# Where a step's third value product stands: behind the key projection, or at the step's end

## The reference

```python
def local_layer(x):                                  # x: 512 x 128 (one sequence)
    q, k, v = split(shift(x) @ Wqkv)                 # 16 heads of width 64
    q, k = rotary(l2norm(q) * qs), rotary_inv(l2norm(k) * ksc)
    sim = 8 * q @ k.T                                # in windows of 32 queries, 64 keys, masked
    x = x + (softmax(sim) @ v) @ Wo
    h = layernorm(shift(x)) * g + b
    a, gate = split(h @ W1 + b1)                     # 2 x 341
    return x + (a * gelu(gate)) @ W2 + b2
```

## Time and profile before

| | us |
|---|---|
| median of 3 runs | 1943.56 (1942.86 to 1945.3) |
| the profiled execution | 1939.44 |
| its span, first to last instruction | 1937.7 |
| TensorE matmuls busy | 1792.5 (93%) |
| VectorE busy | 1538.9 (79%) |
| ScalarE busy | 1360.8 (70%) |
| GpSimd busy | 1280.3 (66%) |

### The profile page before, as it was taken

The page is one execution under the profiler, slowest core; times in us unless marked ns, Lnnn a source line. Parts: engine busy times, 40 slices in busy tenths (PEclk is TensorE's granted clock), DMA queues, the critical chain, the costliest instruction groups (busy, mean ns, idle before and its releaser), DMA issues.

```text
span 1937.7 us, 60121 instructions
## 1 busy us (share of the span) xinstructions
PE 1792.5 (93%) x24400; PEld 1025.6 (53%) x24400; DVE 1538.9 (79%) x2553; ACT 1360.8 (70%) x2863; POOL 1280.3 (66%) x1223
## 2 busy tenths in 40 slices
PE   5898989768999999999999999999999999999996
PEld 3343434355555555555555555555555555555552
DVE  4788888347888888888888888888888888888874
ACT  1354545447888778887787778887788877888771
POOL 4303020147888887887888887888878888878751
PEclk8899999889999999999999999999999999999998
DMA  8000000223533334333344333343333333333320
GB/s 178 27 2 2 2 1 2 66 50 78 114 75 72 79 81 93 86 73 73 75 90 98 76 68 81 81 92 85 73 81 81 89 74 73 85 74 73 70 47 22
DMA packets 137217, 132.64 MB, mean 68 GB/s; under 512 B 79336, under 2 KB 82984, under 8 KB 136616
## 3 DMA queue, kind: packets, MB, share of 16 engines
q1 hardware_dynamic: 136944, 128.81, 29.9%
HBM read 20.94 MB, written 1.05 MB: 11 GB/s over the span
## 4 chain that ended last, share of the span: by engine, by line
POOL 56%; issue 18%; PE 4%; DVE 1%; ACT 1%; POOLq 0%; DVEq 0%; ACTq 0%
POOL prob L1242 9%; POOL kfin L1270 6%; POOL kfin L1267 6%; POOL kfin L1266 6%; POOL qfin L1275 6%; POOL qfin L1274 5%; POOL sumq L1284 5%; POOL kfin L1271 4%; POOL sumk L1262 4%; POOL sumk L1263 3%; POOL lower L1280 1%; PE bank_z L867 1%; PE bank_y L875 1%; PE bank_a L856 1%; PE bank_z L917 0%
## 5 line engine op out<-in xcount | busy, mean ns | idle before, releaser
L1070 ACT ACTIVATE prob<-s_in,lower,rq 128x64 f32<-128x64 f32 x1536 | 537.8, 436 | 0.3
L856 PE MATMUL bank_a<-x_shift,wqk_sb 128*128 128x512 f32 x768 | 364.6, 597 | 5.9 <-ACT sq L1216 4.2
L1056 ACT ACTIVATE zT<-bank_z 128x1024 f32<-128x1024 f32 x192 | 193.1, 1019 | 72.7 <-PE bank_z L867 71.2
L1242 POOL TENSOR_TENSOR prob<-prob,rden 128x1024 f32<-128x1024 f32 x96 | 182.8, 1904 | 89.4 <-DVE rden L1338 83.6
L1270 POOL TENSOR_TENSOR kfin<-rk,kfin 128x512 f32<-128x512 f32 x96 | 122.4, 1275 | 147.9 <-ACT rk L1197 92.6
L856 PEld LDWEIGHTS bank_a<-x_shift,wqk_sb 128*128 128x128 f32 x768 | 144.5, 191 | 139.9 <-issue 127.5
L385 ACT ACTIVATE a_prob<-a_sT 128x1024 f32<-128x1024 f32 x128 | 130.7, 1025 | 103.4 <-PE a_sT L219 101.4
L494 DVE TENSOR_REDUCE a_negmax<-a_max 128x1 f32<-128x512 f32 x256 | 164.7, 685 | 47.9 <-PE a_max L169 44.2
L875 PE MATMUL bank_y<-zT,wvo_low 128*128 128x512 f32 x384 | 187.2, 610 | 0.7 <-ACT zT L1056 0.4
L875 PE MATMUL bank_y<-zT,wvo_high 128*128 128x512 f32 x384 | 187.2, 610 | 0.0
L867 PE MATMUL bank_z<-pT,xk_prev 32*128 32x128 f32 x3072 | 165.1, 284 | 11.3 <-DVE xn L1371 8.0
(11 more groups left out here) (203 smaller groups left out, 4057.9 us busy)
## 6 DMA issues: line engine op xcount, KB each, us to landing
kpad<-kfin SPq DMA_DIRECT2D x384, 128.0 KB, 2.4
qpair<-qfin SPq DMA_DIRECT2D x384, 128.0 KB, 2.4
wqk_sb<-in_wqkv SPq DMA_DIRECT2D x40, 128.0 KB, 2.6
xk_prev<-xk_own SPq DMA_DIRECT2D x24, 192.0 KB, 2.4
ffn_sb<-in_ffn SPq DMA_DIRECT2D x6, 537.5 KB, 4.1
wvo_low<-in_wqkv SPq DMA_DIRECT2D x6, 256.0 KB, 5.6
wvo_low<-in_wo SPq DMA_DIRECT2D x3, 512.0 KB, 6.7
wvo_high<-in_wqkv SPq DMA_DIRECT2D x6, 256.0 KB, 5.0
```

The costliest lines, as they stand in the source:

```text
L856: last = pe.matmul(bank_a[:, half, :], wqk_sb[:, layer_of(u) % 2, part, half, g * P:(g + 1) * P], cols(u), start=True, stop=True)
L1056: return act.activation(out, in_, ACT.Copy)
L1070: last = act.activation(prob[:, n % 2, i, :], s_in[:, n % 2, i, :], ACT.Exp, bias=lower[:, n % 2, i:i + 1], scale=rq[:, n % 2, i:i + 1])
L1242: pool.tensor_tensor(prob[:, e % 2], prob[:, e % 2], rden[:].unsqueeze(2).broadcast_to([P, TPB * GH, 2 * WIN]), ALU.mult).then_inc(pn_ok, 1)
```

## The change

The third value product (hh = 2) of a step moves from behind the key projection to the end of the step, ahead of the fourth. The first call then issues two products and the second call two. Each product is issued as two records. Nothing else changes: no instruction is added or removed, the order of the sums in `bank_y` is the same, and `y_mm` still comes with the fourth product.

```diff
@@ in TensorE's step(s)
                     if h % GROUPS == 0:
                         after(pe, xa_ok, h // GROUPS - 1)
-                    project_out(h, 0, 3)
+                    project_out(h, 0, 2)
...
                     weigh_rows(e)
                 if quarter(h):
-                    project_out(h, 3, 4).then_inc(y_mm, 1)
+                    project_out(h, 2, 4).then_inc(y_mm, 1)
                 if quarter(e):
                     after(pe, z23_ok, e)
```

## The result

The changed kernel takes 1962.19 us (median of 4 runs, 1961.19 to 1964.45), the kernel before 1944.12 us beside it (4 runs). The ratio is 1.0095, with a 95% interval of 1.008 to 1.0109: slower by 18 us. The forecast was 1945.0 us in 1938 to 1951, no change. It was wrong.

A forecast was written before the change was run, and what follows sets the result against it. TensorE's order was taken to set the step, except where other engines hold it. Units +4.2, first steps -3.9 and last steps +1.2 sum to +1.5 us; on a median of 1943.6 that gave 1945, range 1938 to 1951.

The forecast's parts named there:

- C: Third step kind of a four-step unit: sumk ready, 0.86 us kept, another 0.17 us of copy wait goes; -0.52 us.
- D: Fourth step kind of a unit: sumk not waited for, 0.86 us kept against +0.51 at the end; -0.35 us.
- A unit, +0.20: Four steps, one of each kind: +0.56 + 0.51 - 0.52 - 0.35 = +0.20 us; 21 units in steps 12 to 95, +4.2 us.
- A: First step kind of a unit: sumk just ready, no saving counted, L1422 0.05 us late; +0.56 us.
- B: Second step kind of a unit: TensorE already waits for sumk, all 0.86 us turns into waiting; +0.51 us.
- rival 3: In D, the chain from y_mm to L1422 is 0.25 us late instead of 0.05; +5.7 us, 1949; chance 0.10.
- The key sum as an anchor: At L969 in A and B: sumk's chain starts at TensorE's own tail, so the 0.86 us taken out becomes waiting.
- Rival 1: In A and B sumk comes forward, so every step saves the copy's wait; about 1908, half 1927; chance 0.12.
- Rival 2: At the step's end nothing is filled: the moved product costs 0.86 us in each tail; +34 us, 1976; chance 0.06.
- The first steps, -3.9: Steps 4 to 8 gain 3.0 us ahead of the key sum, steps 9 to 11 the rest; bounds 0 and -5.2.
- The last steps, +1.2: Step 96's moved product comes behind a 3.37 us wait, costing 1.0 us; steps 97 to 99 give +0.15.
- Rival 4, the clock: After longer waits in A and B TensorE returns at half clock once a unit; +57 us, 2001; chance 0.02.

The follow-up runs named there:

- before with its blocks moved (first and second): Kernel before plus satisfied waits and repeated score products, 24 then 15 repeats in step 13, shifting 256-instruction block ends: 1962.62 us (1.0079), then 1936.93 us (0.9953).
- VectorE's late order: Kernel before with VectorE's last hidden rows products and output additions put behind the key's products: 1944.8 us (0.9994).
- VectorE's queue cut: VectorE's L1422, L1428 and L1429 on 8 of 512 columns: in the kernel before 1918.61 us (0.9855), in the changed kernel 1911.62 us (0.9818).
- the two late runs: VectorE's last hidden rows products and output additions put behind the key's: in the kernel before 1944.8 us (0.9994), in the changed kernel 1954.85 us (1.0045).
- the mixed order: Kernel before with the third product moved in C and D only: 1943.01 us (0.9993); with block ends shifted, second try, 1929.27 us (0.9914).

## Why the prediction was wrong, step by step

**The step that failed: the sum.** It has terms for units, first and last steps, and treats what lies between the waits as fixed. The 9.6 us of irregular time in steps 12 to 94, pauses at the ends of blocks and the lower clock behind some, are in none of them. The kernel before had them too, in steps 43, 32, 15 and others, 3.7 us in its trace; I read the 1.00 of the earlier trace rows and the list of waits, where L889's 1.8 us of "issue" was too small to be asked about. The change hardly moves the ends: it carries four instructions past the scores, so the end of step 26 stands at 222 in place of 218, that of step 48 at 220 in place of 216. But there the trace of the kernel before has no pause, and that of the changed one 1.58 and 2.06 us, with a product of 0.86 us fewer ahead of the scores. With the ends moved away from the scores, the two orders compare as 1.0004 and 0.9953 of before, a difference of 0.5%, 9.9 us (each has an interval of 0.13 to 0.15%, on different chips; pauses ahead of step 12 are left in both). So of the 18 us about 10 are the order and about 8 the blocks: pauses cost the changed kernel 17.7 us by its runs (1.0095 to 1.0004) and the kernel before 9.1 (1 to 0.9953). Both are 4 to 5 us more than the traces show in steps 12 to 94 (13.0 and 3.7). For the kernel before one reason is that the profiled execution, 4 us faster than the median, was poor in pauses. Steps 4 to 12 are instruction for instruction the same in before, in before with its blocks moved (first and second), and step 10 has no pause in the first trace, 0.95 us in the second and 1.08 us in the third; from L958 of step 4 to that of step 12 they take 114.1, 115.6 and 117.7 us. And at the end 218 in step 26, where before has no pause, the same TensorE order paused 1.35 us with VectorE's late order and 0.84 us with VectorE's queue cut. So part of the 9.6 us between the two traces is chance of the execution; the 8 us rest on medians. That the missing product is what makes the same ends costlier is argued, not shown. For it: the irregular time grows wherever steps are shorter (11.5 us in C and D alone, 20.8 with VectorE's queue cut).

Between the two traces the forecast of +1.5 us and the measured +21.7 differ by 20.2 us: 9.6 irregular time in steps 12 to 94, 2.8 regular time there, 3.7 in the first steps, 2.4 in the last, and 1.7 ahead of step 3, which the change can't have made.

**A unit, +0.20: measured +0.32.** The signs and the kinds are right: A +0.65 (forecast +0.56), B +0.54 (+0.51), C -0.52 (-0.52), D -0.35 (-0.35). The term mis-sized is "two products take 1.72 us": behind `weigh_rows` they take 1.82, so the tail is 0.61 and not 0.51 later. The copy has no part in it, since it ends 0.23 us ahead of the tail's first weight load. The 0.10 us is in the first record behind `weigh_rows`, which the next follows after 0.53 us in place of 0.43, in both kernels; so a lone product there took 0.96 us, and the copy's wait was 1.21 - 0.96 = 0.25 and not 0.35 us. What comes behind the tail is 0.05 to 0.11 us shorter in return. In A `weigh_rows` also starts 0.09 us later: L1422 starts 0.73 us behind the start of the last linear record in place of 0.63, and now directly behind VectorE's own L1415. That is rival 3's chain, at the upper end of the forecast's 0 to 0.1 and not at the 0.25 of the rival. 21 x 0.32 = 6.7 in place of 4.2.

**The key sum as an anchor: right, with the wrong owner.** All 0.86 us turned into waiting in A and B. But the two late runs show that `sumk` can be made early without any gain; the hold is VectorE's queue, which starts at TensorE's own tail. Rival 1 needed this hold to give way and it did so only where VectorE had less to do. Rival 2 is out: C and D came as forecast. (Its 1976 us is 1975 by its own terms with the first and last steps, which changes nothing.)

**The first steps, -3.9: measured about 0.** From L958 of step 4 to that of step 12 it is 114.16 us after and 114.08 before. Steps 4 to 8 gained 0.9 us and not 3.0, with a pause of 0.50 ahead of the scores in step 5; step 10 was to gain 0.52 and lost 1.1, by a pause of 1.27 us. The pauses are half of the 3.7 us error. In the rest the prediction's lower bound came true (GpSimd's loop holds the period): around step 9 TensorE waits 0.34 and 0.55 us for `sumq` and 0.49 us in step 8 for `sumk`, where before has no such wait.

**The last steps, +1.2: measured +3.6** from step 95's L958 on. Step 95 is longer by 0.35. Most of the rest is the clock: the same six records of the last hidden products, in before (4.25 us) and in after (5.46 us):
```profile
1923.49 4.25 PE L1032 MATMUL bank_z<-hid,ffn_sb 128*128 128x512 f32 x6 [3.58 <-DVE hid L1422]
```
```profile
1944.00 5.46 PE L1032 MATMUL bank_z<-hid,ffn_sb 128*128 128x512 f32 x6 [3.58 <-DVE hid L1422]
```
The granted clock there was 0.65 and 0.50, behind the same wait; the six records some 20 us ahead took 2.74 us at 1.00 before and 4.44 at 0.62 after. What decides between the two was not found, and it changes by itself: two kernels that are the same from step 95 on (the change in C and D alone, without and with its blocks moved the second time) took 90.2 and 87.7 us from step 95's L958 to the end.

**Rival 4, the clock:** it came, but in single steps. The 1.45 us waits of step B left the clock at 1.00 in all units but one (step 17, 0.95 us lost); in the trace of the change in A and B alone the lower level came behind the same waits in four (steps 41, 49, 61 and 73, some 0.9 to 1.0 us each). So one such spell costs about 1 us and not the 2.7 of the rival. Behind the pauses of 1.58 and 2.06 us in steps 26 and 48 it fell (behind that of 1.71 us in step 92 it did not), and these two steps lost 3.5 and 2.9 us in all. The Trainium skill, "TensorE: Matmul & The Clock Gate", A second HAM failure mode, says that short idle pauses let the clock swing: in 3 steps of 83 the trace agrees.

## What to carry to other kernels

Ask of "issue" time in the middle of a run of very short TensorE instructions how many instructions lie between two such pauses: a multiple of 256 points to the stream of instructions as the limit, and then the number of instructions is a parameter of its own, which most edits move. Compare two orders only when the pauses are counted apart, and don't take one execution for the kernel's own amount of them; here the mixed order looked like no change (0.9993), and with the blocks' ends out of the way in both it is 0.4% faster (0.9914 to 0.9953). And a wait that ends at an engine whose chain starts from the waiting engine's own last work can't be shortened by taking work out between the two: it pays to shorten the steps that don't wait (C and D), not those that do (A and B).

## What the runs showed of the hardware that I had not expected

- Ends of TensorE's 256-instruction blocks stalled it 0.2 to 2.4 us where 202 or more instructions of the block were score products (256 of them take 1.4 us), not in every such step; with fewer no pause stood within the scores.
- In 104 pauses of fifteen traces TensorE went on 1.2 to 1.6 us behind the landing of a packet of the instruction queue.
- The same instructions in steps 4 to 12 had 0, 0.95 and 1.8 us of pauses in three executions.
- A second end in the same fast run stalls as well, even some instructions behind it: 1.2 us a step with 250 score instructions in the block, nothing with 242 and fewer.
- 2072 matmul records more made a kernel 17.7 us faster (1.0095 to 1.0004), since they moved the ends.
- Satisfied waits ahead of the product at the step's end cost 0.35 us for 10 and 0.56 us for 12, so 0.1 us for one more; up to 13 ahead of each front product of A, B and D cost nothing.
